# Cross attention through DRAM: high parts of keys and queries stored once, strip loads split in two transfers

## What is computed

```python
q = _split_heads(query @ q_w + q_b, B)
k = _split_heads(key @ k_w + k_b, B)
v = _split_heads(value @ v_w + v_b, B)
scores = jnp.einsum('bhqd,bhkd->bhqk', q, k) * SCALE
attn = jax.nn.softmax(scores, axis=-1)
out = jnp.einsum('bhqk,bhkd->bhqd', attn, v)
out = out.transpose(0, 2, 1, 3).reshape(B, -1, EMBED_DIM)
return out @ o_w + o_b
```

## Time and profile before

| | us |
|---|---|
| median of 3 runs | 965.95 |
| lowest, highest | 965.72, 967.9 |
| the profiled execution | 968.62 |
| its span from first to last instruction | 966.8 |
| TensorE busy in it | 830.7 (86%) |
| DVE busy | 594.1 (61%) |
| ACT busy | 449.3 (46%) |
| GpSimd busy | 351.1 (36%) |

### The profile page before, as it was taken

One profiled execution on the slowest core, in us unless ns is written; L12 is line 12 of the kernel. 1 busy time (PEld: TensorE's weight loads), 2 busy tenths in 40 slices (PEclk: granted clock), 3 DMA queues, 4 the chain that ended last, 5 costly groups with the idle time before them and its releaser, 6 DMA issues.

```text
span 966.8 us, 17149 instructions
## 1 busy us (share of the span) xinstructions
PE 830.7 (86%) x6187; PEld 615.1 (64%) x6187; DVE 594.1 (61%) x1431; ACT 449.3 (46%) x831; POOL 351.1 (36%) x321
## 2 busy tenths in 40 slices
PE   7799789779989888984677878988988999999895
PEld 5677557667667665773454545556875777777774
DVE  5799899467888889672645656753552333333265
ACT  5687666446665654531244545665322332222221
POOL 9422201024455447432001344334530142222693
PEclk9999999879999997997678889999998999999998
DMA  5699669898967867356234555306303222221421
GB/s 170 194 276 289 207 178 284 274 227 246 254 161 196 235 189 210 129 179 220 85 135 132 178 164 151 130 30 202 83 23 95 67 66 58 65 66 44 149 64 66
DMA packets 160722, 149.18 MB, mean 154 GB/s; under 512 B 92288, under 2 KB 129216, under 8 KB 159360
## 3 DMA queue, kind: packets, MB, share of 16 engines
q1 hardware_dynamic: 157232, 138.72, 49.2%
q0 software_dynamic: 3408, 9.38, 2.6%
HBM read 86.90 MB, written 61.03 MB: 153 GB/s over the span
## 4 chain that ended last, share of the span: by engine, by line
PE 51%; DVE 12%; ACT 11%; DMA 10%; POOL 8%; issue 5%; SPq 2%; POOLq 0%; DVEq 0%; ACTq 0%
PE ps L2729 10%; PE ps L2744 5%; PE ps L665 4%; DMA q_pad<-staged 4%; DMA queries<-q_pad 3%; PE ps L2593 3%; DVE big L1445 2%; POOL hank L344 2%; PE ps L422 2%; POOL kept L2876 2%; PE ps L2031 2%; PE ps L2104 2%; PE ps L1401 2%; POOL hTlo L2663 2%; PE ps L2606 1%
## 5 line engine op out<-in xcount | busy, mean ns | idle before, releaser
L2154 DVE TENSOR_REDUCE cmx<-ps 128x4 f32<-128x1024 f32 x64 | 77.4, 1219 | 56.6 <-PE ps L2104 56.1
L2729 PE MATMUL ps<-wr,xbT 128*128 x312 | 101.1, 467 | 1.8 <-ACT xbT L2765 1.8
L2191 ACT ACTIVATE cross_room<-ps 128x1024 f32<-128x1024 f32 x64 | 65.6, 1025 | 74.5 <-PE ps L2117 69.1
L2818 POOL DMA_INDIRECT y_dram<-yb,dest_row x39 | 37.5, 961 | 132.7 <-DVE dest_row L2794 128.2
L1361 POOL TENSOR_TENSOR st<-st,exponent 128x20 f32<-128x20 f32 x16 | 56.5, 3533 | 63.6 <-DVE st L1336 61.9
L2729 PEld LDWEIGHTS ps<-wr,xbT 128*128 128x128 f32 x312 | 59.9, 193 | 30.5 <-issue 4.2
L549 DVE SCALAR_TENSOR_TENSOR room<-room 128x256 f32<-128x256 f32 x144 | 58.4, 477 | 11.2 <-ACT room L498 11.2
L2803 DVE TENSOR_TENSOR cross_room<-cross_room,ps 128x352 f32<-128x352 f32 x39 | 20.3, 521 | 60.9 <-PE ps L2729 60.9
L2104 PE MATMUL ps<-keys,queries 49*128 49x256 f32 x224 | 31.7, 364 | 28.1 <-DMA queries<-q_pad 21.1
L2773 ACT ACTIVATE cross_room<-ps 128x352 f32<-128x352 f32 x39 | 18.1, 465 | 74.3 <-PE ps L2729 74.3
L2809 DVE TENSOR_SCALAR yb<-ps,weight 128x256 f32<-128x256 f32 x39 | 18.9, 484 | 50.8 <-PE ps L2744 50.8
(11 more groups left out here) (355 smaller groups left out, 2194.0 us busy)
## 6 DMA issues: line engine op xcount, KB each, us to landing
xs_dram<-staged SPq DMA_DIRECT2D x17, 1040.0 KB, 6.6
room<-in_gW SPq DMA_DIRECT2D x8, 1280.0 KB, 7.4
tok_dram<-room SPq DMA_DIRECT2D x8, 768.0 KB, 6.5
fir_dram<-room SPq DMA_DIRECT2D x6, 1024.0 KB, 7.1
paths<-fir_dram SPq DMA_DIRECT2D x48, 128.0 KB, 3.9
keys<-k_pad SPq DMA_DIRECT2D x28, 196.0 KB
queries<-q_pad SPq DMA_DIRECT2D x28, 196.0 KB
xb<-xs_dram SPq DMA_DIRECT2D x39, 130.0 KB, 2.4
```

Source lines behind the costliest of these rows:

```text
L2154: V.tensor_reduce(mx[:, :, half, :, g].rearrange("p t c -> p c t"), ps[:, pair(h), :].rearrange("p c (t k) -> p c t k", t=TT), AX.X, ALU.m ...
L2191: S.activation(pT[g % 2][:, pair(h)].rearrange("p c k t -> p (c k t)"), ps[:, pair(1 - h), :].rearrange("p c n -> p (c n)"), ACT.Exp, scal ...
L2729: m = nc.tensor.matmul(ps[:, 2 * (j % 2) + half, 0:FF], xbT[j % 2][:, k, :], wr[:, bass.ds(e, 1), k, half, :].rearrange("p e n -> p (e n)" ...
```

## The change

`sp_strips_out` stores each of the two parts once, in two DMAs of 256 KB. In DRAM there are 33 rows for each tensor now: for keys low, high and the row of ones, for queries high, low and the row of zeros. `sp_strips_in` uses two DMAs for what was one: `front` fills the strip's first 32 rows, `back` the last 17. For keys, `front` reads rows 0 to 31 (low, high) and `back` rows 16 to 32 (high again, and the ones). For queries (`twice`), `front` reads rows 0 to 15 twice, as a source with a leading dimension of 2 and a stride of zero, and `back` reads rows 16 to 32. What arrives in SBUF is what arrived before, 196 KB for each half and group. The counts that the semaphores wait for go from 64 to 128.

```diff
-        pg.nc.sync.dma_start(pad[:, ROWS - 1].rearrange("b c g t -> b (c g t)").rearrange("b (p n) -> p b n", p=P),
+        pg.nc.sync.dma_start(pad[:, 2 * XD].rearrange("b c g t -> b (c g t)").rearrange("b (p n) -> p b n", p=P),
...
-def sp_strips_out(pg, pad, twice, once, first, landed):
-
-    rows = lambda part, n: pad[part * XD:(part + n) * XD]
-    pg.nc.sync.dma_start(rows(first, 2).rearrange("(i d) c (u n) t -> (d c u) i (n t)", i=2, n=KT),
-                         flat(twice).unsqueeze(1).broadcast_to([P, 2, KT * T])).then_inc(*landed.up(16))
-    pg.nc.sync.dma_start(rows(2 - 2 * first, 1).rearrange("d c (u n) t -> (d c u) (n t)", n=KT), flat(once)).then_inc(*landed.up(16))
...
+def sp_strips_out(pg, pad, hi, lo, first, landed):
+
+    for part, t in ((first, hi), (1 - first, lo)):
+        pg.nc.sync.dma_start(pad[part * XD:(part + 1) * XD].rearrange("d c (u n) t -> (d c u) (n t)", n=KT), flat(t)).then_inc(*landed.up(16))
...
-def sp_strips_in(pg, strips, pad, half, landed):
+def sp_strips_in(pg, strips, pad, half, landed, twice):
 
     g = slice(half * SLOTS // 2, (half + 1) * SLOTS // 2)
     for c in range(HL):
-        pg.nc.sync.dma_start(strips[c * DH:c * DH + ROWS, g].bitcast(F32), pad[:, c, g]).then_inc(*landed.up(16))
+        front, back = strips[c * DH:c * DH + 2 * XD, g].bitcast(F32), strips[c * DH + 2 * XD:c * DH + ROWS, g].bitcast(F32)
+        first = pad[0:XD, c, g].unsqueeze(0).broadcast_to([2, XD, SLOTS // 2, T]) if twice else pad[0:2 * XD, c, g]
+        pg.nc.sync.dma_start(front, first).then_inc(*landed.up(16))
+        pg.nc.sync.dma_start(back, pad[XD:2 * XD + 1, c, g]).then_inc(*landed.up(16))
...
-                sp.wait_ge(strips_in[i][1], 64 * (b // 2))
+                sp.wait_ge(strips_in[i][1], 128 * (b // 2))
...
-                pe.wait_ge(strips_in[b % 2][half], 64 * (b // 2 + 1))
+                pe.wait_ge(strips_in[b % 2][half], 128 * (b // 2 + 1))
...
-        env.k_pad = nc.dram_tensor("k_pad", [B, ROWS, HL, SLOTS, T], F32).ap()
-        env.q_pad = nc.dram_tensor("q_pad", [2, ROWS, HL, SLOTS, T], F32).ap()
+        env.k_pad = nc.dram_tensor("k_pad", [B, 2 * XD + 1, HL, SLOTS, T], F32).ap()
+        env.q_pad = nc.dram_tensor("q_pad", [2, 2 * XD + 1, HL, SLOTS, T], F32).ap()
```

More of the change, by code:

```diff
@@ L1637, in sp_first_keys @@
             for half in range(2):
-                sp_strips_in(pg, env.first_keys, env.k_pad[0], half, kv.strips_in0[half])
+                sp_strips_in(pg, env.first_keys, env.k_pad[0], half, kv.strips_in0[half], False)
         def sp_first_queries(_):
@@ L1642, in sp_first_queries @@
             for half in range(2):
-                sp_strips_in(pg, env.first_queries, env.q_pad[0], half, kv.strips_in0[half])
+                sp_strips_in(pg, env.first_queries, env.q_pad[0], half, kv.strips_in0[half], True)
         def sp_keep_keys(b):
@@ L1989, in sp_keys_in @@
                 sp_room(b, half)
-            sp_strips_in(pg, kS[home(b)], env.k_pad[b], half, strips_in[b % 2][half])
+            sp_strips_in(pg, kS[home(b)], env.k_pad[b], half, strips_in[b % 2][half], False)
         def sp_query_in(b, half):
@@ L1995, in sp_query_in @@
                 sp_room(b, half)
-            sp_strips_in(pg, qS[home(b)], env.q_pad[b % 2], half, strips_in[b % 2][half])
+            sp_strips_in(pg, qS[home(b)], env.q_pad[b % 2], half, strips_in[b % 2][half], True)
         def sp_lift(b, half):
```

## The result

| | before | after |
|---|---|---|
| median of 4 runs, us | 966.92 | 1114.97 |
| lowest to highest, us | 965.72 to 975.44 | 1111.93 to 1120.2 |
| the profiled execution, us | 968.62 | 1120.2 |

The ratio is 1.151, 95% interval 1.143 to 1.160. The change costs 148 us by the medians and 151.6 by the profiled executions.

The account below looks back on a forecast made before the run. The SBUF-DRAM-SBUF round trip bounds the kernel now, DMA engine 0 after the change. Delays accumulate from +26 at the seam through +49, +51 and +139.5 to +158 us: 968.6 becomes 1126.6, or 1124 on the medians' footing; range 1035 to 1190.

Parts of the forecast that it names:

- (a): Seam of the two phases: last key store lands at 476.4 us instead of 450.2, +26 us.
- (b): Batch 1's keys, query store, query loads and tokens: to 519 us against 469.96, +49 us so far.
- (c): Work, keys, weights and store up to batch 2's query issue: 540.2 us against 489.50, +51 us so far.
- (d): Five batch periods of 43.8 us, the last without weights: 217 us, to 757.3 against 617.78, +139.5 us so far.
- (e): Batch 7's second half, 170 rows: its fifth scores wait until 788.8 us against 630.91, +158 us in all.
- Stores: Strip stores shrink from 768 to 512 KB: 0.66 us less each, about nine on the path, gain 6 us.
- Number of loads: 64 strip loads become 128 at 0.31 us of SP each: up to 4 plus 2.5 us, hidden under engine 0's backlog.
- Shape: Strip loads: 17 rows on one engine, doubled fronts on two; engine 0 gets 208 rows, 36.8 us a batch; the deciding term.
- Fronts on 16 engines: Rival: doubled query fronts spread over 16 engines, 152 rows a batch on engine 0, period 33.9, total 1045 us; chance 0.09.
- small loads taking turns over the engines: Rival: small strip loads use different engines, first half lands 3 us later seven times, total 985 us; chance 0.05.
- an even deal whatever the count: Rival: strip-load rows dealt to all 16 engines, -1.2 us in eight batches, total 956 us, faster; chance 0.06.
- bytes alone: Rival: only the bytes of stores and loads count and cancel with the extra issues, total 966 us; chance 0.02.

Follow-up runs that it names:

- the 16 + 33 kernel: Kernel before with its stores and layout, each load of 49 rows split in 16 and 33 rows: 961.41 us against 971.13, ratio 0.992.
- the kernel with 32 + 17: Kernel before with its stores and layout, each load of 49 rows split in 32 and 17, no zero-stride source: 1054.47 us against 971.13, ratio 1.087.
- the kernel with 16 + 1: Changed kernel with each transfer of 17 rows done as 16 and 1, doubled query front kept: 1014.17 us against 974.04, ratio 1.042.
- The kernel with mended keys: Changed kernel with keys stored twice and loaded as 16 and 33 rows, queries as in the change: 1069.22 us, ratio 1.098.
- the kernel with queries as 16 + 33: Changed kernel with queries read as 16 rows, then 33 from row 0, no zero stride; keys still 32 and 17: 989.94 us, ratio 1.018.

## Why the prediction was right, step by step

1124 was predicted, 1114.97 measured. The mechanism holds: the split of a load in two parts decides, by the number of its rows, over how many DMA engines it is spread. The sizes, by the prediction's own letters; the times of the changed kernel's profile have the 11.4 us of the first phase taken off:

| step | forecast | measured | against before |
|---|---|---|---|
| (a) last key store landed | 476.4 | 481.96 - 11.4 = 470.6 | +20.4, forecast +26 |
| (b) first L2118 (before L2117) | 519 | 523.18 - 11.4 = 511.8 | +41.8, forecast +49 |
| (c) queries of batch 2 issued | 540.2 | 545.52 - 11.4 = 534.1 | +44.6, forecast +51 |
| (d) five periods | 217 | 754.45 - 545.52 = 208.9 | 128.3 before |
| (e) fifth scores of batch 7 | 788.8 | 785.66 - 11.4 = 774.3 | +143.4, forecast +158 |

The row of the last line, and SP's before it:

```profile
754.45 0.64 SPq L851 DMA_DIRECT2D queries<-q_pad  x1
...
785.66 0.80 PE ps L2105 x4
```

So of the 14.5 us by which (e) came earlier than forecast, 7.2 had been gained at the seam by (b), 1.1 were lost again in (c), 8.1 were gained in (d), and the last leg was right, 31.2 us (754.45 to 785.66) for 31.5.

**Part by part.** *Stores:* 0.66 us by bytes agrees with what well cut loads show, 0.4 to 1 us a batch. It is small change here. *Number of loads:* in the changed kernel the additional issues fall under engine 0's queue, as said; in the 16 + 33 kernel, without such a queue, 0.8 us of them shows behind the store of batch 2, and that kernel is faster than before all the same. *Shape:* 17 rows on one engine, by the shares of 0.06 and the kernel with 32 + 17; the doubled front on two engines, by 0.12 to 0.14 and 46 to 52 GB/s; and the same engine for all of them, since otherwise 32 + 17 could not cost 83 us nor keep the share at 0.06 with eight loads issued; the profile names no engine, so which one it is isn't shown.

The Trainium skill, "DMA: Bandwidth & Descriptors", section "Rules for kernel authors", says that a leading zero-stride broadcast of c copies confines a DMA to at most c engines. By that rule, the runs agree: two engines for two copies (0.12 to 0.14), and a load 3.8 us longer in the kernel with 16 + 1. No row of before had shown it.

**The term that was mis-sized** is the price of a row. I took 0.177 us from stretches in which seven engines share the load. One engine with nothing beside it carries 25 to 26 GB/s, which makes 0.158 to 0.164 us for 4 KB; on 1636 rows 0.016 us less are 26 us. But over a whole period, with weights, tokens and stores beside the rows, the measured 41.8 less 5.3 and 1.6 leave 34.9 us for 208 rows, 0.168 each, and the last leg leaves 0.175. The forecast's price was too high by 5% in (d) and right in the last leg. That it came so near is luck in part: it had been read from a state that didn't return, and the lone engine's price would have been as far off the other way. Its sum also has small slips: the terms of (a) add up to 476.7 and those of the period to 43.7. And its reading of the chain is too broad: stores of 7 to 8 us stand on it in batches 2 to 6; batch 1's took 3.45.

**SP held.** The prediction didn't foresee that single issues would take 2 to 4 us, expert weights at line 2406 and the store's own among them; the page has SP's queue at 8% of the chain for 2% before. What this costs is another question. Just before the store of batch 3 lands at 586.64, the share is still one engine's:

```profile
584.00:586.50 2.50, 2.45 (x41) 1.34 (x40) 2.33 (x6) 2.13 (x4) 0.89 (x2) 0.98 0.06 24
```

An engine that has work up to there lost nothing by the late issues in this batch, so "all fall under engine 0's backlog" isn't refuted. A kernel with the same queue and SP free was not run.

**One limit or two.** I called engine 0 "the bound" instead of latency. For the changed kernel that stands: from the issue of batch 2's queries to its first scores are 13.8 us (545.52 to 559.30), to the next store's issue 14.3 (573.65), to the next query issue 13.0 (586.66), and 5.1, 12.2 and 8.5 before; these legs add up to the period by construction, and the two that grew most are those in which a transfer stands in engine 0's queue. From batch 5 on the chain no longer goes over store and first half, but from one batch's second half to the next:

```profile
726.92 19.13 DMA queries<-q_pad
...
766.77 18.84 DMA queries<-q_pad
```

The kernel with mended keys sets both limits apart: engine 0 has work for 29.1 us and the period is 35.6, which is a loop of dependences, with the share at 0.01 before the next queries. So the forecast's step (d) gave nearly the right number for the change, but as a rule, "period = rows of the fullest engine", it is only a lower bound, and it failed by 3.6 us a batch on a kernel close by.

**What the profile was to show.** Waits of the scores' weight loads over 100 us: 128.8. Waits in the middle of a batch: yes, in six. Distance 40 to 47: 41.8. A store over 15 us: no, 14.2 us at the most on the chain (from 614.36), and 13.0 from SP's issue (573.65) to the next step (586.66) in batch 3. DMA share of 0.06 to 0.12 "through most of 450 to 790": only in stretches, for the slices have 1 to 3 tenths, with tokens, weights and the scattered rows moved in between on all engines:

```profile
570.00:790.00 220.00, 120.90 (x890) 76.43 (x890) 82.17 (x204) 68.41 (x102) 44.99 (x52) 0.73 0.24 79
```

**What was left over.** Of the 154.8 us by which the fifth scores of batch 7 are late (785.66 - 630.91) 151.6 are left at the end; 3 us are regained in the experts' phase, and I didn't look for where. Of the 151.6, 11.4 lie ahead of the first key store in this pair of profiles. The medians, whose executions also differ among themselves, say 148.

**The rivals.** Fronts on 16 engines (1045) fell by the share of two engines; small loads taking turns over the engines (985) fell by the kernel with 32 + 17, whose share is one engine's with eight loads issued; an even deal whatever the count (956) and bytes alone (966) fell with the result.

## What to carry to other kernels

Before a transfer is split, padded or given a repeated read, write down for each part the number of rows that both sides have outermost, and its largest divisor up to 16. In the runs here that many engines carried it as far as the shares can tell (7 for 49 rows, 1 for 17, 2 for two copies), and parts with few engines piled up on the same one. 49 as 16 + 33 was 0.8% faster, as 52 it was 1.5% faster (1.2% on a second chip, where no change isn't excluded), as 32 + 17 it was 8.7% slower, with the same bytes or more. A read of overlapping rows by a second transfer does what a stride of zero does, and leaves the engines free. When parts pile up on one engine, count both the engine's total and every loop of waits that runs through its queue, the transfers that the issuing engine stands behind included; a loop can bind where the total doesn't.

## What the runs showed of the chip that I had not expected

- One DMA engine alone, with rows of 4 KB and the other 15 idle, carries 25 to 26 GB/s (share 0.06 to 0.07). Each of seven at once had 20.4 to 25.4 and each of sixteen 24.3, and in the kernel with 52 rows a busy engine had 15.7.
- SP's issuing instruction takes 2 to 4 us for one transfer where many rows are queued on one engine; that the length of the queue holds it is the likely reading, how long it may grow wasn't measured. The clearest row is the back of the first queries, the eighth load in a row. The issues of before in the rows shown are under 0.5 us for one, and the longest single one there between 450 and 620 us is 0.94 (line 1809, at 534.31).

```profile
461.53 3.65 SPq L852 DMA_DIRECT2D first_queries<-q_pad  x1
```

- A query load whose source has the stride of zero takes SP 0.64 us (545.52) where two loads without it take 0.63, so about twice as long for one. In the kernel with queries as 16 + 33 a front without it takes 0.32.
- Executions of the same program differ by 9 us in the first phase, 2.3 of them by a load of hank that TensorE has to wait for. That is more than some of the differences asked about here, so times were compared between marks inside a profile, and whole times only by ratios.
